# The last cross-attention of a decoder layer: exponentials cut into 16-bit halves before instead of after they are turned

## The chip, the cores and the metric

The kernel runs on one core of a Trainium2 chip. The metric is the time of one execution on the device, in microseconds, and the median of several runs. The engines work side by side, each on its own queue of instructions, and meet by semaphores: TensorE (PE in the profile, its weight loads PEld), VectorE (DVE), ScalarE (ACT), GpSimd (POOL) and SyncE (SP), which issues the DMAs.

## What is computed

A decoder layer on x of 4 batches, 512 tokens and 1024 features, all in float32: causal self-attention, cross-attention on a context of 64 tokens, and a gated feed-forward whose weights come as 4-bit codes with scales. Only the cross-attention is touched:

```python
def _L0_xattn_ref(q, k, v, start_pos, mask):          # 32 heads of 32, 8 heads of keys and values
    scores = jnp.einsum('bsgrd,btgd->bgrst', xq, xk) / math.sqrt(HEAD_DIM)
    scores = scores + mask
    probs = jax.nn.softmax(scores.astype(jnp.float32), axis=-1).astype(q.dtype)
    out = jnp.einsum('bgrst,btgd->bsgrd', probs, xv)
    return out.reshape(b, s, N_HEADS * HEAD_DIM)

x = x + _L0_attn_ref(_layernorm(x), ...)
x = x + _L0_xattn_ref(_layernorm(x), ctx_1024, ctx_1024, 0, mask_SxS2_ff0)
x = x + _L0_ffn_ref(_layernorm(x), ...)
```

## The kernel before

All large products are made of 16-bit halves: a float32 value a is cut into high = float16(a) and low = float16(a - high), and a product is the sum of high by high, high by low and low by high.

The program has two parts. The first goes through the self-attention in steps; the cross-attention of batches 0 to 2 rides in these steps, and behind the last step stands the cross-attention of batch 3 alone, a loop over n with 16 units (4 row tiles of 128 tokens by 4 groups of 8 heads) that is called the last cross-attention here. The second part is the feed-forward, in 14 groups, which begins as soon as TensorE has left the loop and VectorE has cut the next to last row (`banks_ready`).

There is no planner: each engine's order is written out by hand, and it is this order that decides who waits. In iteration n of the last cross-attention, with n the unit:

- **TensorE** (`last_cross`): scores of unit n (L1056); weighing of unit n-2 with the values (`x_weigh`, L1075); turn of the exponentials of unit n-1 (`x_turn`, L1063), which are 128 tokens by 8 heads of 64 context tokens, in four float32 transposes of 128x128 into one PSUM bank; the eight float32 transposes of a normalised row (`ln_turn`, L921), if one is due.
- **VectorE**: mask addition (L1456) and maximum (L1460) of unit n; low half of the turned exponentials of unit n-1 (`x_low_part`, L1464), which reads them from PSUM; output of unit n-2 (L1469, L1473); the low halves of a turned row (`ln_low_part`, L1373); normalisation of a row (`ln_normal`, L1367); statistics of a row (`ln_stats`, L1352 to L1357); a few operations for the first feed-forward weights (`look_up`, maxima L277 and differences L283).
- **ScalarE**: high half of the turned exponentials of unit n-1 (`x_high_part`, L1239), out of PSUM; exponential of unit n (`x_exps`, L1235); the high halves of a turned row (`ln_high_part`, L1164); lines and high halves for the weights (L257, L260, L266).
- **GpSimd**: subtraction of the maximum of unit n (`shift`, L822); addition of unit n-2 to the residual (`add_cross`, L829); the root for a row's normalisation (`ln_root`, L802); scaling and low halves for the weights (L294, L299).
- **SyncE** loads codes and scales of the weights and a row.

Rows are the layer-normalised inputs of the next scores and of the feed-forward. `LATE_ROWS` lists the nine of this stage, each with the iterations for statistics, normalisation and turn: turns fall in iterations 2, 5, 6, 8, 9, 12 and 16, normalisations in 1, 4, 5, 7, 8, 11 and 15, statistics in 0, 3, 4, 6, 7, 10 and 14, one before and one after the loop.

In the trace one buffer's name can stand for many views: `p` is p32, the three slots for scores and exponentials, `arena` holds p_h and p_l among others, `pair` and `bank` are PSUM, `w_l` is also the weight lines' buffer, `q_rows` the buffer of the cut weights.

Of the kernel before, what the change touches and what calls it, by code (L numbers as in the profile page):

```python
# [22 lines left out]
P = 128  # L23
# [281 lines left out]
def attention(nc, ctx, block, t, tiles, dram):  # L305
# [50 lines left out]

    bank = t.bank
# [63 lines left out]
    x_exp = sem("x_exp")  # L421
    x_turned = sem("x_turned")
# [376 lines left out]
    def _(pool):  # L799
# [93 lines left out]
        add_cross(LATE_X - 1, x_row[:, 1, :])  # L893
        for n in range(-2, 0):
            make_tiles(tiles.in_turn(tiles.SCALED, n), tiles.in_turn(tiles.LOW, n))
        for n in range(NX + 3):
            x = LATE_X + n
            if n < NX:
                shift(x, p32[:, x % 3, :])
            if 2 <= n < NX + 2:  # L900
                if (n - 2) % 4 == 0:
                    pool.wait_ge(*last_loaded((n - 2) // 4))
                add_cross(x - 2, last_row[(n - 2) // 4])
            for at in late_rows(0, n):
                ln_root(LN_AT[at])
            make_tiles(tiles.in_turn(tiles.SCALED, n), tiles.in_turn(tiles.LOW, n))

    @block.tensor
    def _(pe):
# [155 lines left out]

        def x_weigh(x, dst, high, low):
            n = x % NX
            pe.wait_ge(x_low, x + 1)
# [46 lines left out]
        def last_cross():  # L1115
# [9 lines left out]
            for n in range(NX + 2):  # L1125
# [8 lines left out]
                if n >= 2:  # L1134
                    if n >= 4:
                        pe.wait_ge(x_read, x - 3)
                    x_weigh(x - 2, O_BANK + x % 2, p_h[:, x % 2, 0, :], p_l[:, x % 2, 0, :])
                if 1 <= n <= NX:
                    if n >= 3:
                        pe.wait_ge(x_low, x - 2)  # L1140
                    x_turn(x - 1, T_BANK + (x - 1) % 2, p32[:, (x - 1) % 3, :])
# [13 lines left out]
    def _(act):  # L1155
# [133 lines left out]
        for s in range(FROM, TO):  # L1289
            step(s)  # L1290
            if s < 0:
                for n in range(2):
                    cut_w(4 + 2 * (s - FROM) + n)
        act.wait_ge(x_done, LATE_X - 1)
# [3 lines left out]
        for n in range(NX + 2):  # L1298
# [5 lines left out]
            if 1 <= n <= NX:  # L1304
                if n == 1:
                    act.wait_ge(o_done, NS)
                if n >= 3:
                    act.wait_ge(x_done, x - 2)
                x_high_part(x - 1, T_BANK + (x - 1) % 2, p_h[:, (x - 1) % 2, 0, :])
            if n < NX:  # L1310
                x_exps(x, p32[:, x % 3, :])
            for at in late_rows(2, n):
# [7 lines left out]
    def _(dve):  # L1320
# [224 lines left out]
        for n in range(-2, NX + 4):  # L1545
# [14 lines left out]
            if 1 <= n <= NX:  # L1560
                x_low_part(x - 1, T_BANK + (x - 1) % 2, p_h[:, (x - 1) % 2, 0, :], p_l[:, (x - 1) % 2, 0, :])
# [34 lines left out]
    def last_turn(pe):  # L1596
        for half in range(2):
            pe.wait_ge(ln_xn, last + 1)
            pe.wait_ge(x_low, NX * B)
# [281 lines left out]
```

## Time and profile before

| | before |
|---|---|
| median of 3 runs | 2725.89 us (2719.62 to 2726.89) |
| profiled execution | 2724.36 us, span 2722.6 us |
| granted TensorE clock, mean | 0.976 |
| TensorE busy | 2574.9 us, 95% |
| VectorE busy | 2063.6 us, 76% |
| ScalarE busy | 1547.6 us, 57% |
| GpSimd busy | 1238.8 us, 46% |
| attention and cross-attention | up to 975 us |
| feed-forward | from 975 us on |

The page gives each engine's busy time, then the span in 40 equal slices (68 us each), in which a digit is the busy share in tenths; further parts give the groups of instructions by line. A timeline row says when an instruction started, how long it lasted, on which engine, from which line, what it wrote and read, and in brackets how long its engine had stood idle and for whom. Consecutive instructions of one kind stand in one row with their count. A granted clock of 1.0 is 2.4 GHz on TensorE and 0.5 is 1.2 GHz.

### The profile page before, as it was taken

How to read it: one execution, taken by the hardware profiler on the slowest of the kernel's cores; microseconds unless marked ns; L12 is line 12 of the kernel's file. 1: busy time of each engine (PE TensorE's matmuls, PEld its weight loads, DVE VectorE, ACT ScalarE, POOL GpSimd, SP SyncE). 2: the span in 40 equal slices, each digit the busy share in tenths (PEclk: the TensorE clock that was granted, in tenths of full speed). 3: DMA queues.
4: the chain of work that ended last, by engine and by line, in shares of the span. 5: the costliest groups of instructions: out<-in, count | busy, mean ns of one | idle time of the engine just before them, and what ended most of it. 6: DMA issues, size and time to landing. Idle time of an engine off the chain costs nothing.

```text
span 2722.6 us, 52702 instructions
## 1 busy us (share of the span) xinstructions
PE 2574.9 (95%) x18536; PEld 1399.6 (51%) x18536; DVE 2063.6 (76%) x2860; ACT 1547.6 (57%) x2762; POOL 1238.8 (46%) x1032
## 2 busy tenths in 40 slices
PE   5899999999975589999999999999999999999999
PEld 3577677777764444444444444444444444444444
DVE  5666678778788897878787877878787877878773
ACT  3466666666665465647474655556474746556450
POOL 2356677777775543434252424334242524343340
PEclk9999999999996789999999999999999999999999
DMA  6242443343343132111111111111111111111113
GB/s 197 88 152 95 121 127 123 102 138 117 97 146 118 35 117 75 55 40 62 41 59 46 62 39 54 54 46 54 43 57 46 56 44 62 39 54 54 46 35 123
DMA packets 155421, 212.23 MB, mean 78 GB/s; under 512 B 34576, under 2 KB 86288, under 8 KB 155280
## 3 DMA queue, kind: packets, MB, share of 16 engines
q1 hardware_dynamic: 155280, 210.31, 24.6%
q8 instruction: 93, 1.52, 0.2%
q14 instruction: 48, 0.39, 0.0%
HBM read 163.98 MB, written 44.56 MB: 77 GB/s over the span
## 4 chain that ended last, share of the span: by engine, by line
PE 85%; DVE 6%; DMA 2%; issue 2%; POOL 2%; ACT 1%; SPq 1%; ACTq 0%; DVEq 0%; POOLq 0%
PE bank L1721 43%; PE pair L1740 21%; PE bank L961 6%; PE bank L967 2%; PE pair L1018 2%; PE bank L989 2%; PE bank L921 1%; PE bank L1056 1%; DMA nat_parts<-nat 1%; PE pair L1041 1%; PE pair L1045 1%; PE pair L1043 1%; POOL arena L808 1%; PE bank L991 1%; PE pair L1020 1%
## 5 line engine op out<-in xcount | busy, mean ns | idle before, releaser
L277 DVE TENSOR_TENSOR w_l<-w_l 128x512 f32<-128x512 f32 x1008 | 920.6, 962 | 2.6 <-ACT w_l L260 2.5
L260 ACT ACTIVATE w_l<-proj 128x512 f32<-128x512 int32 x1008 | 592.3, 620 | 417.8 <-DVE w_l L277 300.8
L1721 PE MATMUL bank<-w_h,q_rows 128*128 128x512 f16 x2688 | 586.7, 380 | 0.9 <-issue 0.9
L1740 PE MATMUL pair<-k_rows,arena 128*128 128x512 f16 x2688 | 582.4, 379 | 0.0
L808 POOL TENSOR_TENSOR arena<-p,arena 128x512 f16<-128x512 f32 x320 | 371.7, 1170 | 221.8 <-ACT arena L1231 220.8
L1721 PEld LDWEIGHTS bank<-w_h,q_rows 128*128 128x128 f16 x2688 | 263.3, 98 | 319.2 <-issue 3.4
L1740 PEld LDWEIGHTS pair<-k_rows,arena 128*128 128x128 f16 x2688 | 263.0, 98 | 317.2
L299 POOL TENSOR_TENSOR q_rows<-x1T,q_rows 128x512 f16<-128x512 f32 x112 | 144.8, 1293 | 492.1 <-ACT q_rows L266 492.1
L257 ACT ACTIVATE w_l<-proj,bounds 128x512 f32<-128x512 int32 x336 | 232.1, 714 | 233.7 <-DVE w_l L277 213.6
L294 POOL TENSOR_TENSOR x1T<-x1T,nat 128x512 f32<-128x512 f32 x168 | 266.3, 1585 | 200.6 <-DVE x1T L283 200.6
L1425 DVE TENSOR_REDUCE block_max<-bank 128x4 f32<-128x512 f32 x320 | 218.7, 687 | 160.6 <-PE bank L991 156.9
L1223 ACT ACTIVATE p<-pair 128x512 f32<-128x512 f32 x320 | 190.9, 597 | 246.0 <-PE pair L1020 245.3
L1721 PE MATMUL bank<-w_l,q_rows 128*128 128x512 f16 x1344 | 294.6, 379 | 0.0
L1721 PE MATMUL bank<-xT,q_rows 128*128 128x512 f16 x1344 | 294.6, 379 | 0.0
L1685 POOL TENSOR_TENSOR arena<-p,arena 128x512 f16<-128x512 f32 x112 | 173.5, 1549 | 264.1 <-ACT arena L1764 264.1
L1797 DVE SCALAR_TENSOR_TENSOR arena<-pair,arena 128x1024 f32<-128x1024 f32 x140 | 171.4, 1224 | 121.6 <-PE pair L1740 121.6
L1792 DVE SCALAR_TENSOR_TENSOR p<-bank,p 128x512 f32<-128x512 f32 x112 | 77.4, 691 | 199.9 <-PE bank L1721 199.0
L961 PE MATMUL bank<-xT,w_h 128*128 128x512 f16 x720 | 218.4, 385 | 10.8 <-POOL arena L887 10.8
L1721 PEld LDWEIGHTS bank<-xT,q_rows 128*128 128x128 f16 x1344 | 131.6, 98 | 158.5
L1721 PEld LDWEIGHTS bank<-w_l,q_rows 128*128 128x128 f16 x1344 | 131.6, 98 | 158.5
L1231 ACT ACTIVATE arena<-p 128x512 f16<-128x512 f32 x320 | 192.1, 621 | 0.0
L989 PE MATMUL bank<-k_rows,q_rows 96*128 96x512 f16 (+3 forms) x512 | 135.2, 303 | 20.0 <-DMA q_rows<-nat_parts 10.7
(131 smaller groups left out, 3740.8 us busy)
## 6 DMA issues: line engine op xcount, KB each, us to landing
proj<-in_codes SPq DMA_DIRECT2D x168, 256.0 KB, 3.0
nat<-in_scales SPq DMA_DIRECT2D x336, 128.0 KB, 2.9
nat_parts<-nat SPq DMA_DIRECT2D x48, 256.0 KB, 2.1
q_rows<-nat_parts SPq DMA_DIRECT2D x96, 128.0 KB, 2.7
x_unit<-in_x SPq DMA_DIRECT2D x64, 128.0 KB, 2.7
x<-x_unit SPq DMA_DIRECT2D x64, 128.0 KB, 2.3
xn<-in_x SPq DMA_DIRECT2D x14, 512.0 KB, 4.2
x_row<-x SPq DMA_DIRECT2D x14, 512.0 KB, 4.4
```

Source lines behind the costliest of these rows:

```text
L257: op = self.nc.scalar.activation(self.t.line[:, m, :], self.t.codes[:, slot, :], ACT.Relu, scale=slope, bias=(self.t.above, self.t.below)[ ...
L260: op = self.nc.scalar.activation(self.t.line[:, m, :], self.t.codes[:, slot, :], ACT.Copy, scale=slope, bias=intercept)
L277: self.nc.vector.tensor_tensor(line[:, n + 2, :], line[:, n, :], line[:, n + 2, :], ALU.max)\
L294: self.nc.gpsimd.tensor_tensor(w, w, self.t.scales[:, k % 2, :], ALU.mult).then_inc(self.scaled, 1)
L808: nc.gpsimd.tensor_tensor(p_l[:, n % 2, k, :], p32[:, f % 3, :], p_h[:, n % 2, k, :], ALU.subtract).then_inc(p_low, 1)
L961: mm = nc.tensor.matmul(dst[:, :], w[:, c, cols], xT[:, :, half, c, :], start=(c == 0 and m == 0), stop=(c == CT - 1 and m == 2))
L989: nc.tensor.matmul(dst[:, col:col + keys], t.q_rows[0:96, u % 2, 2 * j + hh, P * qt:P * qt + P], t.k_rows[0:96, u % 2, j, 0:keys], start=T ...
L1223: nc.scalar.activation(p32[:, f % 3, :], bank[T_BANK + T_OF[f % CHUNKS]][:, :], ACT.Exp, scale=SELF_SCALE).then_inc(t_exp, 1)
L1231: nc.scalar.activation(p_h[:, n % 2, k, :], p32[:, f % 3, :], ACT.Copy).then_inc(p_high, 1)
L1425: nc.vector.reduce_max(block_max[:, n % PAIRS, k, :], bank[S_BANK + S_OF[k]][:, :].rearrange("p (a n) -> p a n", n=P), AX_X)\
L1721: mm = nc.tensor.matmul(bank[(GATE, UP)[kind] + n % 2][:, :], w[:, chunk, kind, P * c:P * c + P], t.fT[nb][:, :, part, c, :], start=(m == ...
L1740: mm = nc.tensor.matmul(down_bank[r % 2][:, half, :], h[:, m // 3, rows], w[:, m // 3, cols], start=(m == 0), stop=(m == 5))
```

## The change

In the last cross-attention alone the exponentials are cut before they are turned. ScalarE, right behind the exponential of unit n, copies it as float16 (`e_cut`, high); GpSimd subtracts that from the float32 exponential (`cut_exp`, low), as its first work of iteration n+1, ahead of the shift of unit n+1. TensorE turns both halves in eight 16-bit transposes against a float16 identity (`late_turn`) into one PSUM bank, and ScalarE copies all 1024 columns of that bank out at once (`late_out`). VectorE's low half of the turned exponentials goes. ScalarE's order in an iteration becomes: exponential n, high half n, copy of the turned halves n-1, then the row and the weights; before, the copy of n-1 stood ahead of the exponential of n. The identity lies in the buffer of a mask that is no longer used and is written by one more ScalarE copy ahead of the loop. Weighing waits for `late_out` (`x_high`) in place of the low half (`x_low`).

```diff
--- before.py
+++ after.py
@@ -353,6 +353,11 @@
     w_raw = [w.rearrange("p (c n) -> p c n", c=2) for w in w_raw]
 
     last_row = t.y[RT - QT:]
+
+
+    ident_h = t.mask_qk[:, :].bitcast(FP16)
+    e_cut = [[buf[:, n, 1, :] for buf in (p_h, p_l)] for n in range(2)]
+    e_turned = [p_h[:, n, 2:4, :] for n in range(2)]
 
     bank = t.bank
     S_BANK, PROJ_BANK, T_BANK, O_BANK, XO_BANK = 0, 2, 4, 6, 7
@@ -419,6 +424,9 @@
     x_topped = sem("x_topped")
     x_shifted = sem("x_shifted")
     x_exp = sem("x_exp")
+    ident_cut = sem("ident_cut")
+    e_high = sem("e_high")
+    e_low = sem("e_low")
     x_turned = sem("x_turned")
     x_high = sem("x_high")
     x_low = sem("x_low")
@@ -891,10 +899,19 @@
             step(s)
         ln_root(LN_AT["cross", B - 1, 0])
         add_cross(LATE_X - 1, x_row[:, 1, :])
+        def cut_exp(n):
+            high, low = e_cut[n % 2]
+            pool.wait_ge(e_high, n + 1)
+            if n >= 2:
+                pool.wait_ge(x_turned, LATE_X + n - 1)
+            nc.gpsimd.tensor_tensor(low, p32[:, (LATE_X + n) % 3, :], high, ALU.subtract).then_inc(e_low, 1)
+
         for n in range(-2, 0):
             make_tiles(tiles.in_turn(tiles.SCALED, n), tiles.in_turn(tiles.LOW, n))
         for n in range(NX + 3):
             x = LATE_X + n
+            if 1 <= n <= NX:
+                cut_exp(n - 1)
             if n < NX:
                 shift(x, p32[:, x % 3, :])
             if 2 <= n < NX + 2:
@@ -1063,9 +1080,22 @@
                 mm = nc.tensor.transpose(bank[dst][:, P * i:P * i + P], e[:, P * i:P * i + P], t.ident[:, :])
             mm.then_inc(x_turned, 1)
 
+        def late_turn(n, dst):
+            pe.wait_ge(ident_cut, 1)
+            pe.wait_ge(e_low, n + 1)
+            turned = bank[dst][:, :].bitcast(FP16)
+            for part in range(2):
+                for i in range(4):
+                    mm = nc.tensor.transpose(turned[:, HALF * part + P * i:HALF * part + P * i + P],
+                                             e_cut[n % 2][part][:, P * i:P * i + P], ident_h)
+            mm.then_inc(x_turned, 1)
+
         def x_weigh(x, dst, high, low):
             n = x % NX
-            pe.wait_ge(x_low, x + 1)
+            if x < LATE_X:
+                pe.wait_ge(x_low, x + 1)
+            else:
+                pe.wait_ge(x_high, x + 1)
             if n == 0:
                 pe.wait_ge(vx_laid, 16 * 4 * (x // NX + 1))
             W = 2 * (D + 1)
@@ -1134,11 +1164,11 @@
                 if n >= 2:
                     if n >= 4:
                         pe.wait_ge(x_read, x - 3)
-                    x_weigh(x - 2, O_BANK + x % 2, p_h[:, x % 2, 0, :], p_l[:, x % 2, 0, :])
+                    x_weigh(x - 2, O_BANK + x % 2, *[e_turned[x % 2][:, part, :] for part in range(2)])
                 if 1 <= n <= NX:
                     if n >= 3:
-                        pe.wait_ge(x_low, x - 2)
-                    x_turn(x - 1, T_BANK + (x - 1) % 2, p32[:, (x - 1) % 3, :])
+                        pe.wait_ge(x_high, x - 2)
+                    late_turn(n - 1, T_BANK + (x - 1) % 2)
                 for at in late_rows(2, n):
                     turn(at)
 
@@ -1291,6 +1321,14 @@
             if s < 0:
                 for n in range(2):
                     cut_w(4 + 2 * (s - FROM) + n)
+        def late_out(n, src):
+            act.wait_ge(x_turned, LATE_X + n + 1)
+            nc.scalar.activation(e_turned[n % 2].rearrange("p a n -> p (a n)"), bank[src][:, :].bitcast(FP16), ACT.Copy)\
+                .then_inc(x_high, 1)
+
+        act.wait_ge(scored, CHUNKS * NS)
+        act.wait_ge(o_done, NS)
+        nc.scalar.activation(ident_h, t.ident[:, :], ACT.Copy).then_inc(ident_cut, 1)
         act.wait_ge(x_done, LATE_X - 1)
         x_high_part(LATE_X - 1, T_BANK + XT_OF, px_h)
         for n in range(-2, 0):
@@ -1301,14 +1339,14 @@
                 act.wait_ge(proj_done, NP * B)
                 for half in range(2):
                     ln_high_part(LN_AT["cross", B - 1, 0], half, PROJ_BANK + half, xT[:, 0, :, :, :])
-            if 1 <= n <= NX:
-                if n == 1:
-                    act.wait_ge(o_done, NS)
-                if n >= 3:
-                    act.wait_ge(x_done, x - 2)
-                x_high_part(x - 1, T_BANK + (x - 1) % 2, p_h[:, (x - 1) % 2, 0, :])
             if n < NX:
                 x_exps(x, p32[:, x % 3, :])
+                act.wait_ge(x_exp, x + 1)
+                if n >= 2:
+                    act.wait_ge(x_turned, x - 1)
+                nc.scalar.activation(e_cut[n % 2][0], p32[:, x % 3, :], ACT.Copy).then_inc(e_high, 1)
+            if 1 <= n <= NX:
+                late_out(n - 1, T_BANK + (x - 1) % 2)
             for at in late_rows(2, n):
                 if at[:2] == ("third", B - 1):
                     act.wait_ge(x_scored, LATE_X + 4 * (at[2] + 1))
@@ -1557,8 +1595,6 @@
                 if n >= 3:
                     dve.wait_ge(x_turned, x - 2)
                 x_soft(x, S_BANK + x % 2, p32[:, x % 3, :])
-            if 1 <= n <= NX:
-                x_low_part(x - 1, T_BANK + (x - 1) % 2, p_h[:, (x - 1) % 2, 0, :], p_l[:, (x - 1) % 2, 0, :])
             if 2 <= n < NX + 2:
                 x_out(x - 2, O_BANK + x % 2)
             for at in late_rows(2, n):
@@ -1596,7 +1632,7 @@
     def last_turn(pe):
         for half in range(2):
             pe.wait_ge(ln_xn, last + 1)
-            pe.wait_ge(x_low, NX * B)
+            pe.wait_ge(x_high, NX * B)
             for c in range(4):
                 mm = nc.tensor.transpose(bank[T_BANK + half][:, P * c:P * c + P],
                                          xn[:, xn_slot(*LN_ORDER[last]), P * (4 * half + c):P * (4 * half + c + 1)],
```

## Rows read from the trace of the kernel before

**Rows 1.** The page, busy tenths in 40 slices of the span, TensorE

```profile
PE   5899999999975589999999999999999999999999
```

**Rows 2.** Stretches: us, busy time and instructions by engine, granted clock, DMA share, GB/s

```profile
core 0: us, PE busy (x) PEld busy (x) DVE busy (x) ACT busy (x) POOL busy (x), PEclk, DMA share, GB/s
886.68:974.95 88.27, 49.02 (x402) 39.25 (x401) 78.54 (x147) 41.15 (x75) 45.15 (x45) 0.71 0.10 29
982.00:1060.00 78.00, 78.00 (x367) 35.82 (x366) 67.54 (x76) 59.07 (x107) 39.30 (x27) 1.00 0.40 141
```

**Rows 3.** Timeline, step 6: start us, length us, engine, line, output and inputs [idle before]

```profile
919.77 0.68 DVE L1456 TENSOR_TENSOR p<-bank,arena 128x512 f32<-128x512 f32 x1
...
921.25 1.04 POOL L822 TENSOR_TENSOR p<-p,s_top 128x512 f32<-128x512 f32 x1 [3.22 <-DVE s_top L1460]
...
922.33 0.63 ACT L1235 ACTIVATE p<-p 128x512 f32<-128x512 f32 x1 [3.54 <-POOL p L822]
...
922.86 1.06 ACT L1164 ACTIVATE w_l<-bank 128x512 f16<-128x512 f32 x2
...
923.47 1.29 DVE L1373 TENSOR_TENSOR w_l<-bank,w_l 128x512 f16<-128x512 f32 x2 [1.13 <-ACT w_l L1164]
```

**Rows 4.** VectorE's waits from 888 to 972: us in total, times, longest

```profile
DVE xT L1373 <- ACT xT L1164: 5.2, 5, 1.1
```

**Rows 5.** Timeline of VectorE, steps 13 and 14

```profile
958.68 0.68 DVE L1456 TENSOR_TENSOR p<-bank,arena 128x512 f32<-128x512 f32 x1
...
961.77 0.68 DVE L1456 TENSOR_TENSOR p<-bank,arena 128x512 f32<-128x512 f32 x1
...
963.83 0.69 DVE L1464 TENSOR_TENSOR arena<-pair,arena 128x512 f16<-128x512 f32 x1 [0.65 <-ACT arena L1239]
964.43 0.20 DVE L1469 RECIPROCAL rx_sum<-pair 128x8 f32<-128x8 f32 x1
```

**Rows 6.** Timeline of TensorE, the turns of step 5 (full clock) and step 15 (half)

```profile
916.87 0.63 PE L1063 MATMUL pair<-ident,p 128*128 128x128 f32 x4 [0.66 <-ACT p L1235]
...
970.58 1.09 PE L1063 MATMUL pair<-ident,p 128*128 128x128 f32 x4 [0.37 <-ACT p L1235]
```

**Rows 7.** Timeline of ScalarE, two weight cuts of 1024 columns early in the kernel

```profile
71.10 1.99 ACT L1159 ACTIVATE w_h<-x_row 128x1024 f16<-128x1024 f32 x2
```

**Rows 8.** The page's groups: count, busy us, mean ns, idle before, releaser

```profile
L808 POOL TENSOR_TENSOR arena<-p,arena 128x512 f16<-128x512 f32 x320 | 371.7, 1170 | 221.8 <-ACT arena L1231 220.8
```

**Rows 9.** Timeline of GpSimd and VectorE, end of step 0 and step 1

```profile
892.21 1.60 POOL L299 TENSOR_TENSOR q_rows<-x1T,q_rows 128x512 f16<-128x512 f32 x1
...
892.73 1.64 DVE L277 TENSOR_TENSOR w_l<-w_l 128x512 f32<-128x512 f32 x1
894.29 0.68 DVE L1456 TENSOR_TENSOR p<-bank,arena 128x512 f32<-128x512 f32 x1
...
897.88 0.68 DVE L1456 TENSOR_TENSOR p<-bank,arena 128x512 f32<-128x512 f32 x1
```

**Rows 10.** Timeline of VectorE and GpSimd, steps 7 and 11

```profile
926.92 0.68 DVE L1456 TENSOR_TENSOR p<-bank,arena 128x512 f32<-128x512 f32 x1
...
929.41 0.80 DVE L1367 TENSOR_SCALAR xn<-x_row,mean_var,roots 128x1024 f32<-128x1024 f32 x1
...
951.51 1.19 POOL L829 TENSOR_TENSOR x_unit<-arena,x_unit 128x256 f32<-128x256 f32 x1
...
952.04 1.22 DVE L277 TENSOR_TENSOR w_l<-w_l 128x512 f32<-128x512 f32 x1
```

**Rows 11.** Timeline of GpSimd, the shift of step 4

```profile
909.78 1.04 POOL L822 TENSOR_TENSOR p<-p,s_top 128x512 f32<-128x512 f32 x1
```

**Rows 12.** Timeline of VectorE and TensorE, step 15 and the feed-forward's start

```profile
967.25 0.68 DVE L1456 TENSOR_TENSOR p<-bank,arena 128x512 f32<-128x512 f32 x1
...
971.46 1.91 PE L921 MATMUL bank<-ident,xn 128*128 128x128 f32 x8
...
973.57 1.28 DVE L1373 TENSOR_TENSOR xT<-bank,xT 128x512 f16<-128x512 f32 x2
...
974.95 3.57 PE L1721 MATMUL bank<-w_h,q_rows 128*128 128x512 f16 x8 [0.91 <-issue]
```

## The prediction

> **What bounds the kernel now.** I read the row of TensorE's slices first: nine tenths or more, except for the start and a dip in slices 12 to 15 of 68 us each [rows 1]. The stretches show what the dip is [rows 2]. From the first softmax operation of the last cross-attention (886.68) to the first feed-forward matmul (974.95) are 88.27 us, in which VectorE is busy 78.54, TensorE 49.02 at a granted clock of 0.71, GpSimd 45.15 and ScalarE 41.15. Behind it TensorE is busy 78.00 of 78.00. So the feed-forward is bound by TensorE and not touched, and the change is worth what it does to the start of the first feed-forward matmul. In the 88 us the sixteen steps n are set by VectorE and by the loops that it waits in.
>
> The order of one step is read from step 6, counted from the start S of its mask addition (919.77) [rows 3]: GpSimd's shift starts at S+1.48 and takes 1.04; the exponential runs from S+2.56 to S+3.19; ScalarE goes straight on to the high halves of a turned row (L1164) at S+3.09; VectorE, idle for 1.13, starts their low halves at S+3.70. Steps 2, 5, 6, 8, 9 and 12 have such a row. VectorE's waits of the stage name it: 5.2 us in five waits for L1164, 1.1 at the longest [rows 4], and a sixth alike into another buffer. Those six steps are bound by the chain mask, shift, exponential, row copy; the others by the length of VectorE's own list.
>
> **What the change removes.** 16 low halves on VectorE (0.69 us, but 0.60 from start to start: 963.83 to 964.43 [rows 5]; 9.6 us in all), 16 ScalarE copies of 512 columns, and 64 float transposes, four to a step in 0.63 us at the full clock and 1.09 at half of it [rows 6].
>
> **What it adds.** ScalarE: a 128x512 copy that waits for its own exponential, and one 128x1024 copy out of PSUM for the 128x512 one. GpSimd: a 128x512 subtraction ahead of the next shift, as L808 does it, 1.17 us on average [rows 8]. TensorE: eight 16-bit transposes for four float ones. The 1024-wide copy has no row from PSUM; the nearest are two of that width from SBUF, 1.99 together [rows 7]. Bounds: 0.50, if 16-bit values went twice as fast, and 1.06, what two 512-wide copies out of PSUM take [rows 3]. I take 0.95 from start to start, near the two that have rows, as operations on ScalarE overlap by some 0.05 to 0.1 (0.53 from start to start for 0.63). For the eight transposes the nearest rows are the four float ones: bounds half of 0.63 and twice 1.09, I take 1.0, that of rows 6 at half clock; TensorE has 39 us of idle time in the stage, so this counts in the tail only.
>
> The new waits and what is queued behind them: ScalarE's high copy waits for its exponential, with the wide copy, the turned row and the weight tiles' lines behind it; GpSimd's subtraction waits for the high copy, with the next shift, residual sum, root and tile scaling behind it; TensorE's turn waits for the subtraction, with the turned row and the next score behind it, which has a whole step of lead over VectorE. No DMA moves. The one identity copy on ScalarE stands before the stage and waits for work that ended steps earlier: nothing.
>
> **Steps with a row, the largest term.** The new high copy starts when the exponential has ended: S+3.19+0.04 = S+3.23. The wide copy of the step before follows at +0.53 (the spacing of exponential and L1164 in rows 3), S+3.76; L1164 follows at +0.95, S+4.71, where it was S+3.09. That is 1.62 later, and VectorE, which stands idle there, has the low halves, the next normalisation and the next step's mask addition queued behind it. The removed 0.60 only lengthens the idle time. Six steps x 1.62 = +9.7.
>
> **When the low halves are ready.** The high copy ends at S+3.85, GpSimd's subtraction at about S+5.07, and only then may it shift step n+1. A shift that started at 1.48 is held only in steps shorter than about 3.6 us, or where GpSimd comes late. Step 1 lasts 3.59 (894.29 to 897.88) [rows 9], step 11 is late as told below: in steps 2 and 12, both with a row, the chain starts some 0.55 later, together +1.1.
>
> **Steps without a row.** A removed 0.60 is a gain only if the next VectorE operation can run earlier. In steps 3 and 10 that is a statistics operation that reads one input: -0.6 each, -1.2. In steps 1, 4, 7, 11 and 13 it is a normalisation (L1367) or a maximum (L277), and these stretch where GpSimd works: L277 took 1.22 from 952.04 and ended 0.56 after GpSimd's operation of 951.51 to 952.70 [rows 10]. The shift lies at S+1.48 to S+2.52. In step 7 (S 926.92) the normalisation starts at 929.41, S+2.49, so 0.60 earlier it meets the shift. Steps 1, 7 and 13: 0. In steps 4 and 11 GpSimd is late as well: the shift of step 4 (909.78) follows on other GpSimd work without idle time [rows 11], and the new subtraction comes between. Step 4: +0.2; step 11, where the normalisation and L277 each wait behind one GpSimd operation: +0.65. Step 14: its output waits for the weighing of row 12, which waits for a wide copy that is queued behind exponential and high copy of step 13 (end at 4.7 of step 13; some 1.2 more, by estimate, for TensorE to start and end the weighing: 5.9; step 13 lasts 3.09, 958.68 to 961.77). That is 2.8 into step 14, where the output's first operation stood at 2.66 (964.43), its low halves having waited 0.65 [rows 5]: +0.2.
>
> **Step 0.** Four maxima stand in it, the last one 1.64 long, ending 0.56 after GpSimd's L299 of 892.21 to 893.81 [rows 9]. ScalarE's lines now come 0.53 later and the first subtraction is queued right behind L299. Between 0.53 (only the lines are late) and 1.17 + 0.55 (one maximum waits for the subtraction too); GpSimd already slips in between two maxima here, so I take 1.7.
>
> The Trainium skill has this as a rule: "SBUF — State Buffer", section "SBUF: two separate sides", says that VectorE operations with two SBUF inputs, or in a mode that uses both ports, and a GpSimd operation hold a shared pair of ports exclusively, and that the other one is blocked entirely. By that rule moving the low halves is worse than it looks: VectorE's L1464 reads PSUM and SBUF and blocks nobody, GpSimd's subtraction reads two SBUF tensors. The 1.22 us of L277 agree with it [rows 10]. With no such blocking, steps 0, 1, 4, 7, 11 and 13 would give +0.5 - 5 x 0.6 = -2.5 in place of +2.55, and the sum 5 us less.
>
> **The tail.** From the last mask addition (967.25) to the first feed-forward matmul are 7.70 us, and that matmul starts 0.1 after the last row's low halves (973.57 + 1.28 = 974.85) [rows 12]. Anew: high copy to +3.85, subtraction to +5.07, weighing of 14 to +5.7, turn of 15 to +6.7, then the last row's own eight turns and all that follows them. Now they start at 971.46, 0.88 after the four float turns before them [rows 6], and 3.49 ahead of the feed-forward. Anew they start at +6.6, and 3.3 of the 3.49 stay, since VectorE has no low halves of step 15 to do in between: +9.9. The wide copy of 15 runs beside the row's turns. +2.2.
>
> **Sum.** 9.7 + 1.1 - 1.2 + 0.2 + 0.65 + 0.2 + 1.7 + 2.2 = +14.55 us. The profiled execution took 2724.36 (span 2722.6), 1.5 under the median of 2725.89: 2724.36 + 14.55 = 2738.9. Nothing after 982 has slack to give it back, with TensorE at 78.00 of 78.00. 0.3% of the median, 8.2 us, is about what can be told from no change: slower means above 2734.1, faster below 2717.7.
>
> **Rivals.** (A) VectorE's load is what counts and the added work hides: 16 x 0.60 = 9.6 off, 2714.8. For it: VectorE is busy 89% of the stage. Against it: at six steps it waits for just the engine that gets more work. It decides if the 1.62 were under 0.6, which takes a wide copy that costs nothing. 5%. (B) The size is half: the wide copy takes 0.50, a step with a row costs 0.14 + 0.53 + 0.50 = 1.17 (7.0 in six), the five short steps save 0.60 each, steps 3 and 10 too (-4.2), step 0 costs 0.6, the tail 1.0: +4.4, 2728.8, no change that can be told. 18%. (C) GpSimd becomes the bound: in company its subtractions of this shape took up to 1.60 (L299) [rows 9], 0.43 more, and each catches one VectorE operation for 0.56, in the nine steps without a row: 9 x 0.99 = 8.9 more, 2747.7. For it: 16 x 1.17 = 18.7 us on top of 45.15; against it: even then it idles 24 us. 13%. (D) The stage isn't what holds the feed-forward, its weights are: no effect, 2724 to 2727. Against it: the start 0.1 after VectorE's low halves. 2%.
>
> **How the numbers follow.** The forecast, 62%, has its own range of 2734 to 2745: the wide copy at 1.06 adds 0.7, step 0 at 0.53 takes 1.2, subtractions between 1.1 and 1.6 move steps 4, 11, 12 and the tail by up to 2, waits between engines (some 0.04 each) another 1. With (B) down to 2727 and (C) up to 2750, 8 in 10 hold. Slower: the forecast, (C) and the edge of (B), 75%; the same: the rest of (B), (D) and the forecast's lower edge, 20%; faster: (A), 5%.
>
> **What the profile would show.** Right: the stage takes about 103 us, VectorE's busy time in it falls by 10 while its waits for L1164 grow from 6 to some 20 us in about six waits of 2.8 to 3.5; L1164 of a row starts 4.7 after the mask addition; the feed-forward is as long as before. Wrong: wide copies near 0.6; waits for L1164 of 1.1 as before; long VectorE waits for the output's weighing in ordinary steps, which I priced in step 14 only; or maxima of 1.2 in most steps, which would be (C). A lower granted clock than 0.71 in the stage would show in the turns and scores, which I took as hidden.

## The result and the profile after

| | before | after |
|---|---|---|
| median | 2725.18 us (7 runs) | 2735.88 us (7 runs, 2735.33 to 2741.33) |
| ratio after to before | | 1.0048, 95% interval 1.0032 to 1.0065 |
| profiled execution's span | 2722.6 us | 2737.8 us |
| stage: first mask addition of the last cross-attention to first feed-forward matmul | 88.27 us | 101.80 us |
| up to the stage | 886.68 us | 890.13 us |
| behind it | 1747.65 us | 1745.87 us |

The changed kernel is slower, by 10.7 us in the medians and 15.2 us in the two profiled executions. The stage accounts for 13.5 of these. The 3.45 us ahead of it can't be put down to the change: in the profiles of the experiments below, none of which touches what runs there, the stage began between 881.98 and 897.73 us in the variants of the kernel before, and between 884.07 and 895.88 in those of the changed kernel. The last row, 1.8 us less behind the stage, is explained further down.

The stretches of the changed kernel, which answer to [rows 2] (us, busy us and instructions per engine, granted clock, DMA share, GB/s):

```profile
core 0: us, PE busy (x) PEld busy (x) DVE busy (x) ACT busy (x) POOL busy (x), PEclk, DMA share, GB/s
890.13:991.93 101.80, 51.16 (x466) 42.17 (x465) 73.22 (x131) 57.27 (x91) 63.84 (x61) 0.65 0.09 25
998.00:1076.00 78.00, 78.00 (x364) 35.41 (x363) 68.57 (x79) 60.59 (x108) 39.66 (x27) 1.00 0.41 146
```

VectorE, which was the fullest engine with 78.54 us, has 5.3 us less to do, and the stage is 13.5 longer. ScalarE and GpSimd grew by 16.1 and 18.7 us. The feed-forward is as full as it was. VectorE's waits in the stage (us in total, times, longest), against 5.2 us in five in [rows 4]:

```profile
DVE xT L1411 <- ACT xT L1194: 16.3, 6, 3.4
DVE rx_sum L1507 <- PE pair L1105: 6.0, 7, 1.6
DVE w_l L1411 <- ACT w_l L1194: 3.3, 1, 3.3
```

L1411 and L1194 are the low and high halves of a turned row (L1373 and L1164 of before), L1507 is the first operation of the output (L1469 before). The timeline of step 6, the same step as in [rows 3]:

```profile
927.88 0.69 DVE L1494 TENSOR_TENSOR p<-bank,arena 128x512 f32<-128x512 f32 x1
...
929.37 1.04 POOL L830 TENSOR_TENSOR p<-p,s_top 128x512 f32<-128x512 f32 x1 [3.69 <-DVE s_top L1498]
...
930.44 0.63 ACT L1265 ACTIVATE p<-p 128x512 f32<-128x512 f32 x1 [4.03 <-POOL p L830]
931.10 0.63 ACT L1347 ACTIVATE arena<-p 128x512 f16<-128x512 f32 x1
931.64 1.00 ACT L1326 ACTIVATE arena<-pair 128x1024 f16<-128x1024 f16 x1
932.54 1.07 ACT L1194 ACTIVATE w_l<-bank 128x512 f16<-128x512 f32 x2
933.16 1.29 DVE L1411 TENSOR_TENSOR w_l<-bank,w_l 128x512 f16<-128x512 f32 x2 [3.31 <-ACT w_l L1194]
```

Shift and exponential start 1.49 and 2.56 us after the mask addition, as before. Then the high copy (L1347) and the wide copy (L1326) stand where the row's copy stood, and L1194 starts at 4.66 where it started at 3.09. VectorE idles for 3.31 where it idled for 1.13.

The lengths of the sixteen steps, from mask addition to mask addition, the last one to the first feed-forward matmul. They are differences of the start times in the two timelines; R marks the steps in which a turned row is copied:

```
step       0    1    2R   3    4    5R   6R   7    8R   9R   10   11   12R  13   14   15R
before   7.61 3.59 5.50 4.72 5.43 6.24 7.15 5.46 6.23 5.51 4.71 4.35 5.50 3.09 5.48  7.70
after    8.88 3.49 7.83 4.12 5.53 7.90 8.73 5.32 7.90 7.08 4.12 5.39 7.09 3.00 5.59  9.83
change   1.27 -.10 2.33 -.60  .10 1.66 1.58 -.14 1.67 1.57 -.59 1.04 1.59 -.09  .11  2.13
forecast 1.70 0    2.17 -.60  .20 1.62 1.62 0    1.62 1.62 -.60  .65 2.17 0     .20  2.20
```

(In the last line the 1.1 us for late shifts are shared out to steps 2 and 12.) This table is the measure of the experiments too. It is much finer than the time: most steps that an experiment doesn't touch repeat to 0.02 us from profile to profile, while executions differ by several us. Steps 5 and 8 move by up to 0.1. Step 14 moves more, as VectorE waits there for what TensorE turned, and TensorE's clock isn't always the same: it took 5.48 us before, at a granted clock of 0.50, and 5.01 in the kernel before with GpSimd's work added (a run below), at 1.00 in its first 3 us. The turn, first before (VectorE's wait behind it is the 0.65 in [rows 5]), then in that run, with the wait:

```profile
962.01 1.09 PE L1063 MATMUL pair<-ident,p 128*128 128x128 f32 x4 [0.66 <-ACT p L1235]
```

```profile
958.90 0.63 PE L1068 MATMUL pair<-ident,p 128*128 128x128 f32 x4 [0.66 <-ACT p L1240]
960.25 0.69 DVE L1469 TENSOR_TENSOR arena<-pair,arena 128x512 f16<-128x512 f32 x1 [0.19 <-ACT arena L1244]
```

So a difference of up to 0.5 us in step 14 says nothing by itself. Five of the experiments (the narrow subtraction, the half copy, GpSimd's work alone, VectorE's order, and the row ahead of the exponential in the changed kernel) ran once, and only their step lengths are used.

### The profile page after: what moved, and what is told of

Same layout as the page of the kernel before. It is cut to its first block, busy times and chain, and to the rows that moved or that the text cites. A ratio compares the mean times of both kernels' runs of the same rounds, so it can differ in the third digit from the quotient of the medians.

```text
span 2737.8 us, 52863 instructions
## 1 busy us (share of the span) xinstructions
PE 2581.6 (94%) x18600; PEld 1404.2 (51%) x18600; DVE 2064.4 (75%) x2844; ACT 1563.5 (57%) x2779; POOL 1255.4 (46%) x1048
## 4 chain that ended last, share of the span: by engine, by line
PE 84%; DVE 5%; POOL 3%; DMA 3%; issue 2%; ACT 2%; SPq 1%; ACTq 0%; DVEq 0%; POOLq 0%
PE bank L1757 42%; PE pair L1776 21%; PE bank L978 7%; PE bank L984 2%; PE bank L1006 2%; PE pair L1035 2%; PE bank L938 1%; DMA nat_parts<-nat 1%; PE bank L1073 1%; PE pair L1058 1%; PE pair L1062 1%; PE pair L1060 1%; POOL arena L816 1%; PE bank L1008 1%; PE pair L1037 1%
```

## The experiments

### The row right behind the exponential

```diff
             if n < NX:
                 x_exps(x, p32[:, x % 3, :])
+            for at in late_rows(2, n):
+                ...
+                    ln_high_part(LN_AT[at], half, PROJ_BANK + half, t.fT[at[1]][:, at[2], :, :, :])
+            if n < NX:
                 act.wait_ge(x_exp, x + 1)
...
             if 1 <= n <= NX:
                 late_out(n - 1, T_BANK + (x - 1) % 2)
-            for at in late_rows(2, n):
-                ...
```

> The changed kernel with one thing moved back: in an iteration ScalarE copies the turned row right behind the exponential, where it stood before the change, and only then makes the high copy and the wide copy. All added work stays. 'Stage' is the time from the first mask addition of the last cross-attention to the first feed-forward matmul: 88.3 us before, 101.8 after the change. Theory (the row's copy is late because it is queued behind 0.14 + 0.53 + 0.90 us of new ScalarE work): steps 2, 5, 6, 8, 9 and 12 lose the 1.6 us that they gained, L1194 starts at 3.1 after the mask addition again and VectorE waits 1.1 to 1.8 for it; stage about 92, time some 9.5 us under the changed kernel, 2726. Rival (GpSimd's subtraction and the longer way through it to the turns set the steps): stage 100 to 102, the same time as the changed kernel, since that way gets longer still.

The stage took 100.50 us, the time was 1.0055 of before (1.0037 to 1.0073): no gain. Steps 2, 5, 8 and 12 were 2.6, 1.7, 1.7 and 2.0 over before; only step 6 fell to its old length and step 9 half way. My theory failed here as a statement of what would come back, and the timeline of step 5 (mask addition at 922.38) says why:

```profile
924.14 1.04 PE L1089 MATMUL pair<-mask_qk,arena 128*128 128x128 f16 x8
...
924.98 1.91 PE L938 MATMUL bank<-ident,xn 128*128 128x128 f32 x8
...
926.08 0.60 ACT L1194 ACTIVATE xT<-bank 128x512 f16<-128x512 f32 x1 [0.42 <-PE bank L938]
...
928.12 1.15 POOL L907 TENSOR_TENSOR arena<-p,arena 128x512 f16<-128x512 f32 x1 [1.17 <-ACT arena L1353]
928.17 1.66 DVE L1406 TENSOR_SCALAR xn<-xn,mean_var,roots 128x1024 f32<-128x1024 f32 x1
```

ScalarE now waits for TensorE: the row's turns (L938) stand behind the turns of the exponentials (L1089), which stand behind a weighing and a subtraction, so the row's copy starts at 3.7 and not at 3.1. And the subtraction (L907), moved back with the high copy, now starts 0.05 us ahead of VectorE's normalisation, which lasts 1.66 instead of 0.80. Of the 1.6 us that the step should have lost, 0.6 is left in the later start of the copy, 0.25 in a second wait between the row's two halves and 0.9 in the stretched normalisation. Behind the wait that I named, two others are nearly as long.

### ScalarE's new work alone, in the kernel before

```diff
             if n < NX:
                 x_exps(x, p32[:, x % 3, :])
+                act.wait_ge(x_exp, x + 1)
+                nc.scalar.activation(p_h[:, n % 2, 1, :], p32[:, x % 3, :], ACT.Copy).then_inc(extra, 1)
+                nc.scalar.activation(p_h[:, n % 2, 2:4, :].rearrange("p a n -> p (a n)"),
+                                     p_l[:, n % 2, 2:4, :].rearrange("p a n -> p (a n)"), ACT.Copy).then_inc(extra, 1)
             for at in late_rows(2, n):
...
```

> The kernel before with only ScalarE's added work put in: behind each exponential of the last cross-attention a 512-wide copy that waits for it and a 1024-wide copy of 16-bit values, both into unused buffers, read by nobody. VectorE keeps its low halves, GpSimd and TensorE are as before. Theory: six row steps longer by 1.6 (9.6), step 0 by 0.5, step 14 by up to 0.8 as the following copy out of PSUM comes late, nothing in the tail; stage 98.4 to 99.2, time about 10 us over the kernel before. Rival (GpSimd's subtraction): stage 88 to 90, no difference to be measured.

Stage 101.13 us, ratio 1.0064 (1.0047 to 1.0081). Steps 5, 6, 8, 9 and 12 grew by 1.60, 1.61, 1.62, 1.61 and 1.62, within 0.02 of what the sum had; steps 1, 3, 7, 10 and 13 by 0.00 or 0.01. Nothing of GpSimd's, TensorE's or VectorE's part of the change is in this kernel. So the queue on ScalarE alone is enough for the growth of the row steps, though the first experiment shows that it isn't the only thing that holds them. The stage is 2 us longer than the upper end of what I expected: steps 4 and 11 grew by 0.34 each and the tail by 0.70, where I had booked nothing, and step 2 grew by 2.29. Step 2's ScalarE timeline tells of a cause that I hadn't seen:

```profile
904.46 0.63 ACT L1236 ACTIVATE p<-p 128x512 f32<-128x512 f32 x1 [2.65 <-POOL p L823]
905.13 0.63 ACT L1314 ACTIVATE arena<-p 128x512 f16<-128x512 f32 x1
905.66 1.04 ACT L1315 ACTIVATE arena<-arena 128x1024 f16<-128x1024 f16 x1
906.61 0.71 ACT L257 ACTIVATE w_l<-proj,bounds 128x512 f32<-128x512 int32 x1
907.23 0.61 ACT L260 ACTIVATE w_l<-proj 128x512 f32<-128x512 int32 x1
907.75 0.61 ACT L266 ACTIVATE q_rows<-x1T 128x512 f16<-128x512 f32 x1
908.26 0.58 ACT L1240 ACTIVATE arena<-pair 128x512 f16<-128x512 f32 x1
908.74 0.62 ACT L1236 ACTIVATE p<-p 128x512 f32<-128x512 f32 x1
```

There is no idle time from one exponential to the next: in the short step 1 ScalarE has more work than the step lasts, and the exponential of step 2 starts late. The changed kernel shows the same row of operations without a gap in this place.

### GpSimd's subtraction made narrow

```diff
-            nc.gpsimd.tensor_tensor(low, p32[:, (LATE_X + n) % 3, :], high, ALU.subtract).then_inc(e_low, 1)
+            nc.gpsimd.tensor_tensor(low[:, 0:8], p32[:, (LATE_X + n) % 3, 0:8], high[:, 0:8],
+                                    ALU.subtract).then_inc(e_low, 1)
```

> The changed kernel with GpSimd's subtraction cut to 8 of 512 columns; most of the low halves are left out and what is turned in their place is stale. All waits and the order stay. Theory: only what was booked on the subtraction comes back: step 0 from +1.3 to about +0.5, steps 2 and 12 some 0.5 each, step 11 some 1.0 and the tail some 1.1; the row steps 5, 6, 8 and 9 stay 1.6 over before. Stage about 98. Rival (GpSimd is the bound, directly or by stretching VectorE's operations): steps 5, 6, 8 and 9 fall too, stage 90 to 93.

Stage 99.68 us, 2.1 less than the changed kernel. Step 0 fell to +0.31 and step 11 from +1.04 to +0.14, about as booked. The row steps 5, 6, 8 and 9 stayed at +1.58 or +1.59, against the rival. But steps 2 and 12 didn't fall (2.33 and 1.59) and the tail hardly did (2.05 for 2.13), where I had expected 0.5, 0.5 and 1.1: step 2 is ScalarE's backlog just shown, and in the tail the turn of step 15 stands on TensorE behind the weighing of step 14, which waits for a wide copy and is the later of the two.

### The copy out of PSUM at half its width

```diff
-            nc.scalar.activation(e_turned[n % 2].rearrange("p a n -> p (a n)"), bank[src][:, :].bitcast(FP16), ACT.Copy)\
+            nc.scalar.activation(e_turned[n % 2][:, 0, :], bank[src][:, :].bitcast(FP16)[:, 0:HALF], ACT.Copy)\
```

> The changed kernel with the copy out of PSUM cut from 1024 to 512 columns; the low halves are not copied out, so what is weighed in their place is stale. Theory: the 0.90 from start to start falls to about 0.5, so each of the six row steps is 0.4 shorter, the step after a short step too; stage 99.0 to 99.4. Rival (the row's copy waits for its turn on TensorE, which comes late, and not for ScalarE's queue): no change of the row steps, stage 101.5 to 102.

Stage 98.40 us. The six row steps went down by 0.42 to 0.61 from the changed kernel's, five of them by 0.42 or 0.43, and all others but 14 (0.42) and 15 (0.21) by 0.01 at the most. A row step follows the width of this copy one for one, by 0.43 us for 512 columns, and the rival (no change) is out.

### GpSimd's new work alone, in the kernel before

```diff
+            if 1 <= n <= NX:
+                pool.wait_ge(x_exp, x)
+                nc.gpsimd.tensor_tensor(p_l[:, (n - 1) % 2, 1, :], p32[:, (x - 1) % 3, :], p_l[:, (n - 1) % 2, 2, :],
+                                        ALU.subtract).then_inc(extra, 1)
             if n < NX:
                 shift(x, p32[:, x % 3, :])
...
                 if n >= 3:
                     dve.wait_ge(x_turned, x - 2)
+                    dve.wait_ge(extra, n - 2)
```

> The kernel before with only GpSimd's added work put in: a 128x512 subtraction from float32 and 16-bit values ahead of each shift of the last cross-attention, once the exponential of the step before has ended, into an unused buffer that only a later buffer reuse waits for. Theory: step 0 longer by 0.6 to 1.2, steps 4 and 11 by about 1 each, where GpSimd is late, and here and there 0.6 where the subtraction meets a normalisation or a maximum; the row steps otherwise as before: stage 91 to 92.5. Rival (GpSimd's work is what made the change slow): stage 97 or more.

Stage 89.48 us: 20 us more of GpSimd's busy time (65.33 for 45.15) cost 1.2 us, less than I expected. Step 5 grew by 0.71, step 11 by 0.41, step 12 by 0.30, the others by 0.1 or less, step 0 not at all; step 14 was 0.47 shorter, by the clock, as told above, so that at one clock the cost is some 1.7. In step 5 the subtraction meets a normalisation, which takes 1.42 for 0.80. ScalarE's part alone costs step 0 0.46, this part nothing, both together 1.27. The timelines of the changed kernel, and under them of this one, show the difference:

```profile
894.54 4.54 DVE L277 TENSOR_TENSOR w_l<-w_l 128x512 f32<-128x512 f32 x3 [0.77 <-ACT w_l L260]
895.37 1.61 POOL L299 TENSOR_TENSOR q_rows<-x1T,q_rows 128x512 f16<-128x512 f32 x1
...
896.94 1.59 POOL L907 TENSOR_TENSOR arena<-p,arena 128x512 f16<-128x512 f32 x1
899.01 0.68 DVE L1494 TENSOR_TENSOR p<-bank,arena 128x512 f32<-128x512 f32 x1
```

```profile
889.08 1.60 POOL L901 TENSOR_TENSOR arena<-p,arena 128x512 f16<-128x512 f32 x1
889.59 0.68 DVE L1461 TENSOR_TENSOR p<-bank,arena 128x512 f32<-128x512 f32 x1
```

With ScalarE's lines on time the fourth maximum has got in before the subtraction; with the lines late (0.77 of idle time) it comes behind it, and VectorE goes on 0.5 after the subtraction's end.

### The order on VectorE: statistics ahead of the normalisation

```diff
             if n >= 0:
+                for at in late_rows(0, n):
+                    turn_stats(at)
                 for at in late_rows(1, n):
                     ln_normal(LN_AT[at], turn_row(at))
-                for at in late_rows(0, n):
-                    turn_stats(at)
```

> The changed kernel with VectorE's order changed in the steps that have both: statistics ahead of the normalisation (steps 4 and 7), the same instructions. Theory (the removed low half is no gain in step 7 because the normalisation, 0.80 long when alone, lasts 1.27 beside GpSimd's shift, and 1.17 in step 4): after the statistics the normalisation no longer meets the shift, it lasts 0.8 and step 7 falls from 5.32 to 4.85; step 4 from 5.53 by up to 0.4, less if it meets the next subtraction; all other steps within 0.1. Rival (a long normalisation is noise or costs the same wherever it stands): both steps unchanged.

Step 7 fell from 5.32 to 4.86, as expected. Step 4 rose by 0.08, where I had expected up to 0.4 less: there the normalisation still takes 1.22 beside GpSimd's next operations. (Step 14 fell by 0.20 and steps 5 and 8 by 0.10, which is what they move by in other runs too.) In step 7 of the changed kernel the normalisation meets the shift; in this run it doesn't. First the changed kernel, then this one:

```profile
938.18 1.04 POOL L830 TENSOR_TENSOR p<-p,s_top 128x512 f32<-128x512 f32 x1
...
938.50 1.27 DVE L1405 TENSOR_SCALAR xn<-x_row,mean_var,roots 128x1024 f32<-128x1024 f32 x1
```

```profile
934.05 0.81 DVE L1405 TENSOR_SCALAR xn<-x_row,mean_var,roots 128x1024 f32<-128x1024 f32 x1
```

The same instruction takes 1.27 us, ending 0.55 after GpSimd's, or 0.81. Only in this order is the removed low half a gain in step 7: 0.60 of 0.60, where the change as it is gets 0.14.

### The row ahead of the exponential on ScalarE

```diff
+            for at in late_rows(2, n) if n < NX else []:
+                ...
+                    ln_high_part(LN_AT[at], half, PROJ_BANK + half, t.fT[at[1]][:, at[2], :, :, :])
             if n < NX:
                 x_exps(x, p32[:, x % 3, :])
...
-            for at in late_rows(2, n):
+            for at in late_rows(2, n) if n >= NX else []:
```

First in the changed kernel:

> The changed kernel with the same move: ScalarE copies a turned row ahead of the step's exponential. In the run with the row right behind the exponential the row was not turned before 3.7 us after the mask addition in steps 2, 5, 8 and 12, since on TensorE it follows the weighing (behind the wide copy) and the turn (behind GpSimd's subtraction). Theory (after ScalarE's queue the next thing late is TensorE's): the row's copy still starts near 3.7, the exponential of those steps now waits behind it until about 4.8, everything after the exponential is later, stage 98 to 102. Rival (ScalarE's queue alone is to blame): row steps shrink to 5 us, stage about 84.

Stage 95.49 us, between theory and rival. Steps 5 and 8 stayed at 7.98 and 8.04: there the row is turned late, and in step 5 its copy starts 3.70 after the mask addition, as the theory said. But steps 6 and 9 fell to 5.98 and 3.69; each follows a long step, and there the row had been turned earlier. Steps 3, 10 and 13 paid back 0.46, 0.75 and 1.05 of that. Then in the kernel before:

> The kernel before with one thing moved: ScalarE copies a turned row (L1164) ahead of the step's exponential instead of behind it; the same instructions otherwise. Theory (VectorE's wait in a row step is the queue on ScalarE, not the turns on TensorE): TensorE has the row turned around the step's mask addition, so the waits of 0.7 in step 2 and 1.1 in 5, 6, 8, 9 and 12 go: stage 88.3 less 6.3 is 82.0, time about 6 us under the kernel before (ratio 0.9977). Rival (the turns are only just in time, the exponential now waits behind the row and holds the rest): stage 87 to 90, no difference.

Stage 82.93 us and a ratio of 0.9981 (0.9970 to 0.9993): faster than the kernel before by some 5 us (2 to 8 by the interval; in the stage 5.3, for the expected 6.3). Steps 6, 8 and 9 lost 1.2 each, 5 lost 0.67 and 12 lost 0.53. Step 2 lost nothing. Step 14 lost 0.46, but that is TensorE's clock (1.00 there, 0.50 before), not the move, which leaves 4.9 of the stage's 5.3 us. VectorE's waits for a turned row are gone from the list:

```profile
DVE p L1461 <- PE bank L1056: 1.6, 1, 1.6
DVE arena L1469 <- ACT arena L1239: 1.3, 3, 0.7
```

### The row first on TensorE too

```diff
+                for at in late_rows(2, n):
+                    turn(at)
                 if 1 <= n <= NX:
...
-                for at in late_rows(2, n):
-                    turn(at)
```

In the changed kernel, with ScalarE's move:

> The changed kernel with the row ahead on both engines: ScalarE copies it ahead of the exponential, and TensorE turns it ahead of the turn of the exponentials' halves, right behind the weighing. All work of the change stays. Theory (the row steps were long because the row stood behind the new work on ScalarE and on TensorE): the row is turned within 2 us of the mask addition and VectorE hardly waits; the six row steps take 4 to 5.5 us, 28 in all against 46.5 in the changed kernel; stage about 83, time about 8 us under the kernel before (ratio 0.997). Rival (GpSimd's subtraction, its blocking of VectorE and the longer way to the weighing take over as the bound): row steps of 6 or more, stage 92 to 96, time 4 to 8 us over the kernel before.

Stage 91.77 us, ratio 1.0018 (1.0008 to 1.0028): 10 us less than the changed kernel, but 3.5 over before, and 0.2 from the rival's range. The row steps took 34.5 us together, against 46.5 in the changed kernel and the 28 expected. The tail grew to 11.40. And the kernel before with both moves:

> The kernel before with the row ahead on both engines: the row's copy ahead of the exponential (as in the run of that alone, stage 82.9) and on TensorE the row's turn ahead of the turn of the exponentials. Theory (in step 5, which fell by 0.67 only, the row is turned just in time): step 5 falls by another 0.4 and step 2 by up to 0.1; stage 81.5 to 82.5, ratio to the kernel before about 0.9975, not to be told from the run with ScalarE's move alone. Rival (the turns of the exponentials, now behind the row, hold the weighing as in the changed kernel with the same order, where the tail grew by 1.6): stage 84 to 86.

Stage 90.75 us, ratio 1.0019 (1.0008 to 1.0031): the rival's side, and worse than it said. Step 5, which should have lost another 0.4, rose by 0.14 against the run with ScalarE's move alone; steps 2, 6, 9 and 12 rose by 1.2 to 1.7 and the tail by 1.7. With TensorE's row first, the turns of the exponentials come late, and VectorE waits for their copy (from 897.73 to 988.48; before, 1.7 in three):

```profile
DVE arena L1469 <- ACT arena L1239: 8.5, 6, 2.5
```

while TensorE itself stands 6.0 us in seven waits for normalised rows that it used to take up later (before, 3.6 in two):

```profile
PE bank L921 <- DVE xn L1372: 6.0, 7, 2.3
```

So in the kernel before TensorE's order was right as it was, and this move costs 7.8 us there (90.75 against 82.93, of which 0.46 is step 14 with its clock). In the changed kernel the same move gains 3.7 (91.77 against 95.49). Of the two kernels with both moves, the one with the change's work has a stage only 1.0 us longer; with the best order tried for each, it is 8.8 (91.77 against 82.93).

## Why the prediction was right, and where not

The forecast was 14.55 us more stage and 2738.9 us in time; measured were 13.53 and 2735.88 us in the median. The table shows where the terms are off: by 0.58 in step 12, 0.43 in step 0, 0.39 in step 11, and by 0.16 or less elsewhere. That the profiled execution took 2739.58, within 0.7 us of the forecast, is luck: it holds the 3.45 us ahead of the stage and lacks 1.8 behind it, and neither was in the sum.

**The largest term** was 1.62 us in each of six row steps. Measured in 5, 6, 8, 9 and 12: 1.66, 1.58, 1.67, 1.57 and 1.59. Its parts held too: in step 6 the high copy starts 0.66 after the exponential (0.67 in the sum), the wide copy 0.54 after that (0.53), the row's copy 0.90 after that (0.95). ScalarE's work alone gives the same 1.6 in the kernel before. What the sum didn't say is that the way through GpSimd and TensorE was nearly as late: putting the row back behind the exponential brought back 1.3 us of the stage and not 9.7. The sum needed only the longest wait, so it came out right; the remedy that I drew from it didn't.

**Late shifts (+1.1)** were not what set the steps. In step 2 of the changed kernel (mask addition at 902.50) the shift is late as forecast, behind the subtraction:

```profile
903.43 1.15 POOL L907 TENSOR_TENSOR arena<-p,arena 128x512 f16<-128x512 f32 x1 [1.40 <-ACT arena L1347]
904.54 1.04 POOL L830 TENSOR_TENSOR p<-p,s_top 128x512 f32<-128x512 f32 x1
905.81 0.62 ACT L1265 ACTIVATE p<-p 128x512 f32<-128x512 f32 x1
```

It starts 2.04 after the mask addition, 0.56 late. But ScalarE comes later still: with the weights' work of step 1 it is busy until the exponential starts, 0.2 after the shift's end. Step 2 has its extra 0.7 without any subtraction (+2.29 with ScalarE's work alone), and keeps it with a narrow one. So its cause is ScalarE's backlog in step 1, which the sum didn't have, and that 0.7 lies so near to the booked 0.55 is luck. In step 12 the extra didn't come: its shift started 1.49 after the mask addition (at 967.91), not late at all, since the delay had already gone into step 11 (+1.04 for +0.65).

**Removed low halves.** -0.60 and -0.59 in steps 3 and 10, where statistics follow; -0.10, -0.14 and -0.09 in 1, 7 and 13, where an operation that GpSimd holds up follows. The forecast had -0.60 and 0, and the changed order of statistics and normalisation confirms the reason for step 7; for steps 1 and 13 it is argued from the likeness. The rule of the Trainium skill on the shared pair of ports ("SBUF — State Buffer", "SBUF: two separate sides") agrees with 1.27 against 0.81 us for one normalisation. VectorE's busy time fell by 5.3 and not by the 10 of the forecast's last part, since an operation that GpSimd holds up shows as a longer one: the 17 maxima of the stage have a mean of 999 ns, 867 before (2.2 us in all), and the seven normalisations took 1.3 us more in all. The rest of the difference is not accounted for.

```profile
L277 DVE TENSOR_TENSOR w_l<-w_l 128x512 f32<-128x512 f32 x17 | 16.8, 999 | 0.8 <-ACT w_l L260 0.8
```

**Step 0** cost 1.27, between the bounds of 0.53 and 1.72; it takes both new works to get there. **Step 14** has +0.11 for +0.20, but that is no confirmation: before, TensorE's granted clock was 0.50 all through it, and in the changed kernel 1.00 in its first 1.5 us and 0.5 to 0.6 behind. **The tail** cost 2.13 (forecast 2.2), on the way that the sum went, through the weighing of step 14, its turn behind it and the row's turns:

```profile
985.94 1.01 ACT L1326 ACTIVATE arena<-pair 128x1024 f16<-128x1024 f16 x1
...
987.72 1.04 PE L1089 MATMUL pair<-mask_qk,arena 128*128 128x128 f16 x8
988.56 1.91 PE L938 MATMUL bank<-ident,xn 128*128 128x128 f32 x8
...
990.35 1.48 DVE L1411 TENSOR_TENSOR xT<-bank,xT 128x512 f16<-128x512 f32 x2 [1.73 <-ACT xT L1194]
```

**"Nothing after 982 has slack"** missed 1.8 us. TensorE was full there, but not at one clock. The first 24 matmuls of the feed-forward, before and after:

```profile
974.95 7.13 PE L1721 MATMUL bank<-w_h,q_rows 128*128 128x512 f16 x24 [0.91 <-issue]
```

```profile
991.93 5.34 PE L1757 MATMUL bank<-w_h,q_rows 128*128 128x512 f16 x24 [0.80 <-issue]
```

Before, the granted clock was 0.50 (1.2 GHz) in the first 3.0 us from there, and TensorE had been at 0.50 through the whole tail; it rose within the next 3.0. In the changed kernel it was 1.00 (2.4 GHz) from the first matmul on, after 0.53 in the 3 us ahead. Of the twelve profiles six began the feed-forward at the full clock, with 24 matmuls in 5.34 us: the changed kernel and three of its variants, and two variants of the kernel before. Six began it at half, with 6.69 to 7.66: the kernel before, two of its variants, and three of the changed kernel's, so the two kinds of kernel can't be told apart by it. As far as the runs show it is where the clock's changes happen to fall, and it is in no term of the sum; 13.5 - 1.8 = 11.7 us is what the change gave in this profile, in line with the ratio's 8.7 to 17.7.

**The signs.** The stage took 101.80 us for about 103. VectorE's waits for L1194 grew from 6.3 to 19.6 us in seven waits, six of them of 2.5 to 3.4 and one of 1.7 in the tail, and L1194 starts 4.66 after the mask addition for 4.7. Waits for the output's weighing did appear, 6.0 us in seven. But those in the row steps 2, 5 and 12 only take from the wait for L1194 behind them, those in 4 and 11 are of 0.24, and the two long ones are in step 14, where one was booked, and in the tail. The clock in the stage was lower than before, 0.65 for 0.71; what that costs outside step 14 and the start of the feed-forward no run separates.

**The rivals.** (A), VectorE's load decides, is out: it fell and the stage grew. (B), half the size, hung on a wide copy of 0.50; it takes 0.90. (C), GpSimd as the bound, is out by its work alone (+1.2) and by the narrow subtraction (-2.1). What remains of it is 0.7 in step 5, 0.4 in step 11 and 0.3 in step 12. (D), the weights hold the feed-forward, is out: its first matmul came 13.5 us later with the stage. Left open is how much of the changed kernel's row steps each of the two nearly equal ways would hold if the other were gone: only one combination of orders was tried for that, and it brought its own cost.

## What to carry over

Price an operation by the queue that it is put into at the moment when somebody waits behind it, not by the load of the engine that it leaves: here the fullest engine lost 16 operations and its idle time grew from 9.7 to 28.6 us, as the work went ahead of the one copy that it was idle for. Look for the second wait before believing in a remedy; moving the row's copy ahead of the exponential on ScalarE was worth 5 us in the kernel before and 6 in the changed one, and moving it only to right behind the exponential 1.3. A table of the step lengths from the timeline told apart 0.1 us in most steps, where the time told apart some 5, but a step that waits for TensorE has to be compared at one clock.

## What of the hardware was unexpected

- Eight 16-bit transposes of 128x128 span as long as four float32 ones did: 0.61 us (at 983.86, granted clock 1.00) and 1.04 (at 987.72, granted clock 0.50) against 0.63 and 1.09 [rows 6]. I had bounds from half to twice of that.
- A ScalarE copy of 1024 16-bit columns out of PSUM takes 1.00 us, 0.90 from start to start, so 16-bit values go no faster through it than 32-bit ones: two 512-wide float copies take 1.06.
- VectorE's and GpSimd's collisions go both ways: beside a normalisation of VectorE that began first (900.32), GpSimd's shift took 1.54 us where it takes 1.04 alone.

```profile
900.32 0.81 DVE L1405 TENSOR_SCALAR xn<-x_unit,mean_var,roots 128x1024 f32<-128x1024 f32 x1
900.49 1.54 POOL L830 TENSOR_TENSOR p<-p,s_top 128x512 f32<-128x512 f32 x1 [1.95 <-DVE s_top L1498]
```
